# Two graph attention layers and a third: the first layer's bias moves from a product on TensorE to ScalarE's passes over the turned head

## The reference, cut to what matters

```
x = layernorm(x + gat2(elu(gat1(x)) ))       # block 0
x = layernorm(x + leaky(attention(x @ W) @ (x @ W)))   # block 1

gat(x):  xl   = (x @ W).reshape(N, H, F)
         e    = leaky_relu(asrc[s, h] + adst[d, h]), -1e9 where there is no edge
         attn = softmax over the sources s
         out  = sum over s of attn[s, d, h] * xl[s, h, :]   + bias
```

## Time and profile before

| what | value |
|---|---|
| median of 3 runs | 977.99 us (976.63 to 978.44) |
| the profiled execution, its own time | 977.93 us |
| span of the profiled execution | 976.1 us |
| TensorE busy (matmul) | 882.8 us, 90% |
| VectorE busy | 740.5 us, 76% |
| ScalarE busy | 684.9 us, 70% |
| GpSimd busy | 276.1 us, 28% |
| chain that ended last, by engine | TensorE 36%, VectorE 29%, ScalarE 24%, issue 9%, GpSimd 2% |

### The profile page before, as it was taken

How to read it: one execution, slowest core, us unless ns; L and a number is a source line. 1 busy time by engine, 2 the same in 40 slices (tenths; PEclk the granted TensorE clock), 3 DMA queues, 4 the chain that set the end, 5 groups by cost and what they waited for, 6 DMA issues and landing times.

```text
span 976.1 us, 17256 instructions
## 1 busy us (share of the span) xinstructions
PE 882.8 (90%) x6220; PEld 820.9 (84%) x6220; DVE 740.5 (76%) x1876; ACT 684.9 (70%) x1269; POOL 276.1 (28%) x255
## 2 busy tenths in 40 slices
PE   5687889999999999999999999999999999998653
PEld 4676879998999989898999989898999989897542
DVE  5657697888888887888888888888888888974430
ACT  2466858787786868787786868777786868775530
POOL 1001001124242314224242314224242314224353
PEclk9997999999999999999999999999999999999787
DMA  6303030202102030302102030302102010000000
GB/s 205 111 3 87 1 87 2 87 1 63 48 28 82 22 87 1 109 1 64 46 28 82 22 88 1 108 2 65 45 29 80 23 23 1 23 1 23 22 22 22
DMA packets 62716, 45.04 MB, mean 46 GB/s; under 512 B 35748, under 2 KB 54308, under 8 KB 62632
## 3 DMA queue, kind: packets, MB, share of 16 engines
q1 hardware_dynamic: 62632, 43.93, 15.3%
HBM read 27.14 MB, written 8.39 MB: 36 GB/s over the span
## 4 chain that ended last, share of the span: by engine, by line
PE 36%; DVE 29%; ACT 24%; issue 9%; POOL 2%; POOLq 0%; DMA 0%; SPq 0%; DVEq 0%; ACTq 0%
DVE junk L749 9%; PE bU L478 7%; PE bU L457 7%; PE bG L540 6%; PE bG L526 6%; ACT att L620 6%; ACT att L609 6%; ACT x L632 5%; DVE att L793 3%; PE bB L417 3%; DVE y_lo L786 3%; DVE low L762 3%; DVE y L774 3%; ACT att L624 2%; PE bU L468 2%
## 5 line engine op out<-in xcount | busy, mean ns | idle before, releaser
L749 DVE CUSTOM_DVE_ANT_0 junk<-mask_t,bA,val 128x512 bf16<-128x512 bf16 x320 | 219.8, 743 | 44.7 <-PE bA L417 38.2
L457 PE MATMUL bU<-val,att 128*128 128x129 f32 x2048 | 249.7, 275 | 3.3 <-DVE att L793 3.3
L457 PEld LDWEIGHTS bU<-val,att 128*128 128x128 f32 x2048 | 241.5, 192 | 5.7 <-issue 3.4
L793 DVE SCALAR_TENSOR_TENSOR att<-mask_n,att 128x2048 f32<-128x2048 bf16 x80 | 183.4, 2292 | 81.3 <-ACT att L620 81.3
L609 ACT ACTIVATE att<-bB,val 128x512 f32<-128x512 f32 x320 | 202.4, 707 | 1.3 <-PE bB L417 1.3
L620 ACT ACTIVATE att<-att 128x2048 f32<-128x2048 f32 x80 | 155.2, 1940 | 0.7
L478 PE MATMUL bU<-val3s,att 128*128 128x256 f32 x512 | 118.0, 385 | 11.8 <-POOL val3s L372 11.3
L468 PE MATMUL bU<-val,att 128*128 128x257 f32 x512 | 119.9, 388 | 9.4 <-DVE att L793 9.4
L478 PEld LDWEIGHTS bU<-val3s,att 128*128 128x128 f32 x512 | 96.2, 192 | 27.0 <-issue 13.4
L468 PEld LDWEIGHTS bU<-val,att 128*128 128x128 f32 x512 | 96.6, 194 | 23.7 <-DVE att L793 9.9
L672 ACT COPY val<-bG 128x524 f32<-128x524 f32 x64 | 38.7, 604 | 108.6 <-PE bG L540 108.6
(11 more groups left out here) (87 smaller groups left out, 1585.4 us busy)
## 6 DMA issues: line engine op xcount, KB each, us to landing
adj_in<-in_adj_dram SPq DMA_DIRECT2D x16, 1024.0 KB, 5.8
x_in<-in_x_dram SPq DMA_DIRECT2D x16, 512.0 KB, 6.7
out_dram<-act SPq DMA_DIRECT2D x16, 512.0 KB, 2.9
mask_t<-mask_n SPq DMA_TRANSPOSE x64, 2.5
att<-in_L_gnn_W_dram SPq DMA_DIRECT2D x4, 128.0 KB, 3.1
att<-in_L_gnn_W_dram SPq DMA_DIRECT2D x1, 512.0 KB, 7.4
w<-in_L_gnn_W_dram SPq DMA_DIRECT2D x1, 256.0 KB, 7.6
att<-in_L_gnn_a_dram SPq DMA_DIRECT2D x1, 256.0 KB, 7.3
```

The source lines that it names most:

```text
L457: ins = nc.tensor.matmul(to[:, (d % 2) * FX:(d % 2 + 1) * FX], p[:, s, d * P:(d + 1) * P], val1[u.batch % 2][:, s, u.index // 2, values], ...
L749: nc.vector.tensor_tensor_reduce(junk[:, b] if u.row else att[u.slot % 3][:, b], mask_t[u.batch % 4][:, b], bA[:], 1.0, a_col(u, b) if u.r ...
L793: nc.vector.scalar_tensor_tensor(flat(p), mask_n[u.batch % 3][:, 0:NB * N], BIG, flat(p), ALU.add, ALU.min)\
```

## The change

The bias product goes, and with it `ones_r`, the prepared rows and `shift_bias_1`. The bias is loaded as one column per head (`bias1`, 128 x 4) by a DMA late in SP's queue. GpSimd writes the column of ones into val1 once per batch (`set_ones`), and the attention product of a head waits for it. The turning now takes the plain normalized head x1, two slots behind instead of three, at the end of TensorE's slot, after the second half of the product. ScalarE then reads the turned head from PSUM twice, with the bias as a column: exponential into e1 and rectified into r1 (`elu_parts`, three slots behind, at the end of the slot). VectorE's `elu` makes y1 = min(e1, 1) + r1, which is already turned. High and low part are made from y1 in SBUF, four slots behind. y1 has one buffer instead of two, and the bank of a turned head is freed by r1 instead of y_lo.

```diff
         u_uses = [(colsum_out, 2)]
         for g in range(FIRST, LAST + 1):
-            u, older = units.get(g - 1), head_at(g - 3)
+            u, older = units.get(g - 1), head_at(g - 2)
...
             if u:
-                u.use = len(u_uses), len(u_uses) + len(halves[0]) + (older is not None)
-            u_uses += halves[0]
+                u.use = len(u_uses), len(u_uses) + len(halves[0])
+            u_uses += halves[0] + halves[1]
             if older:
                 older.turn_use = len(u_uses)
-                u_uses.append((y_lo_ready, older.h + 1))
-            u_uses += halves[1]
+                u_uses.append((r1_done, older.h + 1))
@@ SP
-            b1_row = b1.rearrange("(o n) -> o n", o=1)
-            sp.dma_start(b1_in[0:1, :], b1_row).then_inc(b1_loaded, 16)
-            sp.dma_start(b1_in[32:33, :], b1_row).then_inc(b1_loaded, 16)
...
+            with nc.allow_non_contiguous_dma(reason="a column for each head"):
+                sp.dma_start(bias1[:], b1.rearrange("(h p) -> p h", p=P)).then_inc(b1_loaded, 16)
             sp.dma_start(bias2[:], b2.rearrange("(o a) -> o a", o=1).to_broadcast([P, DO])).then_inc(w23_in, 16)
@@ GpSimd
-            nc.gpsimd.memset(ones_r[:].bitcast(F32), 1.0).then_inc(consts, 1)
-            nc.gpsimd.memset(bias1[:].bitcast(F32), 0.0).then_inc(const0, 1)
...
+            def set_ones(n):
+
+                pool.wait_ge(val1_ready, (n + 1) * NB)
+                columns = val1[n % 2][:].rearrange("p b g n -> p (b g) n")[:, :, 0:HC].rearrange("p q (c n) -> p q c n", n=FX)
+                nc.gpsimd.memset(columns[:, :, :, F:FX], 1.0).then_inc(ones_ready, 1)
...
+                if pos == 0 and 0 <= n < B:
+                    set_ones(n)
@@ TensorE
             def turn_head(u):
                 to = u_bank(u.turn_use)
-                pe.wait_ge(y1_done, u.h + 1)
+                pe.wait_ge(x1_done, (u.h + 1) * NB)
...
                 pe.wait_ge(prob_done, u.r + 1)
+                pe.wait_ge(ones_ready, u.batch + 1)
...
-                    nc.tensor.matmul(to, ones_r[:], bias1[:, g], start=True, stop=False)
...
                 if before:
                     attend(before, 0)
-                if oldest:
-                    turn_head(oldest)
                 if after and after.row:
                     targets_row(after)
...
                 if before:
                     attend(before, 1)
+                if older:
+                    turn_head(older)
                 if later:
                     sources_row(later)
@@ ScalarE
-            def elu_exp(u):
-                act.wait_ge(x1_done, (u.h + 1) * NB)
+            def elu_parts(u):
+
+                act.wait_ge(x1_turned, u.h + 1)
+                act.wait_ge(b1_loaded, 16)
                 if u.h:
                     act.wait_ge(y1_done, u.h)
-                nc.scalar.activation(e1[:], x1[u.h % 2][:], ACT.Exp, bias=neg_one[:]).then_inc(e1_done, 1)
+                turned, bias = bU[u.turn_use % 4][:], bias1[:, u.index:u.index + 1]
+                nc.scalar.activation(e1[:], turned, ACT.Exp, bias=bias).then_inc(e1_done, 1)
+                nc.scalar.activation(r1[:], turned, ACT.Relu, bias=bias).then_inc(r1_done, 1)
 
             def high_part(u):
-                act.wait_ge(y_turned, u.h + 1)
+                act.wait_ge(y1_done, u.h + 1)
...
-                nc.scalar.copy(y_hi[:, u.index], bU[u.turn_use % 4][:]).then_inc(y_hi_ready, 1)
+                nc.scalar.copy(y_hi[:, u.index], y1[:]).then_inc(y_hi_ready, 1)
...
+                turned = head_at(g - 4)
...
+                if turned and pos == 2:
+                    high_part(turned)
                 if this:
                     leaky(this, (0, 1))
...
-                if oldest:
-                    high_part(oldest)
+                if turned and pos != 2:
+                    high_part(turned)
                 if pos == 4 and third:
                     values_3_out(n - 2, (2, 3))
-                if older:
-                    elu_exp(older)
+                if oldest:
+                    elu_parts(oldest)
@@ VectorE
             def elu(u):
                 dve.wait_ge(e1_done, u.h + 1)
-                if u.h >= 2:
-                    dve.wait_ge(y_turned, u.h - 1)
-                nc.vector.scalar_tensor_tensor(y1[u.h % 2][:], e1[:], 1.0, x1[u.h % 2][:], ALU.min, ALU.max)\
-                    .then_inc(y1_done, 1)
+                dve.wait_ge(r1_done, u.h + 1)
+                if u.h:
+                    dve.wait_ge(y_lo_ready, u.h)
+                nc.vector.scalar_tensor_tensor(y1[:], e1[:], 1.0, r1[:], ALU.min, ALU.add).then_inc(y1_done, 1)
...
-                nc.vector.tensor_tensor(y_lo[:, u.index], bU[u.turn_use % 4][:], y_hi[:, u.index], ALU.subtract)\
-                    .then_inc(y_lo_ready, 1)
+                nc.vector.tensor_tensor(y_lo[:, u.index], y1[:], y_hi[:, u.index], ALU.subtract).then_inc(y_lo_ready, 1)
...
-            shift_bias_1()
             fold_1()
...
-                if last_head:
-                    low_part(last_head)
+                if turned and pos == 2:
+                    low_part(turned)
...
-                if oldest and pos != 1:
-                    low_part(oldest)
-                if older:
-                    elu(older)
+                if turned and pos != 2:
+                    low_part(turned)
+                if oldest:
+                    elu(oldest)
                 if pos == 1 and 0 <= n - 2 < B:
                     norm_stats(n - 2, 0, res1, res1_done, NB, stats1, moments1)
```

More of the change, by code:

```diff
@@ L114, in gat_kernel @@
         e1 = sb("e1", [P, N])
-        y1 = [sb(f"y1_{i}", [P, N]) for i in range(2)]
+        r1 = sb("r1", [P, N])
+        y1 = sb("y1", [P, N])
         y_hi = sb("y_hi", [P, KH, N], F32R)
@@ L335, in _ @@
             nc.gpsimd.memset(val2[:, :, DX:DX + 1], 1.0).then_inc(consts, 1)
-            pool.wait_ge(const0, 2)
-            nc.gpsimd.memset(bias1[0:1, :, 0:HC].rearrange("p g (c n) -> p g c n", n=FX)[:, :, :, F:FX].bitcast(F32), 1.0)\
-                .then_inc(consts, 1)
+            pool.wait_ge(const0, 1)
             nc.gpsimd.affine_select(out=ident[:], in_=ident[:], compare_op=ALU.not_equal, fill=1.0, base=0,
                                     pattern=[[-1, P]], channel_multiplier=1).then_inc(consts, 1)
-            pool.wait_ge(consts, 8)
+            pool.wait_ge(consts, 6)
             nc.gpsimd.tensor_scalar(ident_big[:], ident[:], BIG, 1.0, ALU.mult, ALU.mult).then_inc(consts, 1)
-            pool.wait_ge(consts, 9)
+            pool.wait_ge(consts, 7)
             def norm_scale(m, which, moments_sem, var_sem, rstd_sem):
@@ L536, in values_1 @@
                     to = g_bank(g)[:, 0:HX]
-                    nc.tensor.matmul(to, ones_r[:], bias1[:, g], start=True, stop=False)
                     for k in range(KD):
                         for i, (left, right) in enumerate(((x_hi, w1_hi), (x_hi, w1_lo), (x_lo, w1_hi))):
-                            ins = nc.tensor.matmul(to, left[:, k, nodes], right[:, k, g], start=False,
-                                                   stop=(k == KD - 1 and i == 2))
+                            ins = nc.tensor.matmul(to, left[:, k, nodes], right[:, k, g],
+                                                   start=(k == 0 and i == 0), stop=(k == KD - 1 and i == 2))
                     g_free[g] = ((val1_ready, n * NB + b + 1),)
@@ L545, in weight_sums @@
             def weight_sums():
-                pe.wait_ge(folded, 2 * KD * H + G + 2 * KH)
+                pe.wait_ge(folded, 2 * KD * H + 2 * KH)
                 for k in range(KH):
@@ L692, in _ @@
                 if g == -1:
-                    act.wait_ge(folded, 2 * KD * H + G + 2 * KH)
+                    act.wait_ge(folded, 2 * KD * H + 2 * KH)
                     nc.scalar.copy(w2_hi[:], w2).then_inc(w2_hi_ready, 1)
                 third_layer = units.get(g - 2) if pos == 2 else None
+                if turned and pos == 2:
+                    high_part(turned)
                 if this:
@@ L856, in fold_1 @@
                                         w1_hi[:].rearrange("p k g n -> p (k g n)"), ALU.subtract).then_inc(w1_lo_ready, 1)
-            def shift_bias_1():
-                dve.wait_ge(consts, 9)
-                dve.wait_ge(b1_loaded, 32)
-                for g in range(G):
-                    to_hi, to_lo = (bias1[q:q + 1, g, 0:HC].rearrange("p (c n) -> p c n", n=FX)[:, :, 0:F] for q in (0, 32))
-                    from_hi, from_lo = (b1_in[q:q + 1, g * HW:(g + 1) * HW].rearrange("p (c n) -> p c n", n=F)
-                                        for q in (0, 32))
-                    nc.vector.tensor_scalar(to_hi, from_hi, 1.0, None, ALU.add).then_inc(bias1_ready, 1)
-                    nc.vector.tensor_scalar(to_lo, from_lo, 1.0, None, ALU.add).then_inc(folded, 1)
-                    folds[0] += 1
-                    dve.wait_ge(folded, folds[0])
```

(3 more changed lines are left out.)

24 lines of the change are left out of this document (11 added, 13 removed).

## The result

The changed kernel takes **1029.1 us** (1025.5 to 1030.8, 4 runs) against 977.7 (976.6 to 978.4, 4 runs) of the kernel before: ratio 1.052, interval 1.051 to 1.054. The prediction had the sign and the two waits, but forecast +21 where the profiled spans show 1029.0 - 976.1 = +52.9. It lies well outside the range of 980 to 1006.

A forecast was written before the change was run, and what follows sets the result against it. TensorE was taken as nearly the bound (busy 53.6 of 55 us); per batch +1.75-0.86+0.73 = +1.62, 21.8 over the batches, last fourth quarter +0.6, start and batch 1 -1.5, total +20.9: 998.8 us, range 980 to 1006.

The forecast's parts named there:

- the two waits: TensorE waits 2.0 us for the rectified pass at layer 2's fourth quarter, about 1.3 for b_t at head 2's targets row.
- M4 to M5: Stretch from values_3's end to layer 2's fourth quarter: bank held until the rectified pass ends, 1.75 us more per batch.
- M1 to M3: Stretch from values_1's end to head 3's targets row: VectorE's elu ahead of the statistics, 0.73 us more per batch.
- M2: Mark on TensorE's queue: targets row of head 2, forecast to move from 7.38 to 8.5 us behind values_1's end.
- M1: Mark on TensorE's queue: end of values_1 of block 0, where the second half of the third layer's product starts.
- M3 to M4: Stretch from head 3's targets row to the end of values_3 of blocks 2 and 3: no change, within 0.05 us.
- M5 to M1: Stretch from layer 2's fourth quarter to values_1's end: shorter gap at the targets row, two products gone, 0.86 us less.
- The start: Before the steady part: two loads leave SP's queue, -0.6 us, and eight uncovered products go, -1.8 us.
- the first three: Rivals: only TensorE's work counts (961 us, 8%); only the bank waits (984, 10%); only VectorE's order waits (976.5, 6%).
- the shared port: Rival: a GpSimd operation holds VectorE's low part of head 3 by 1.0 us each batch; 1013 us, 4%.
- M4: Mark on TensorE's queue: end of values_3 of blocks 2 and 3.
- M5: Mark on TensorE's queue: start of the fourth quarter of layer 2's product.

The follow-up runs named there:

- e1_fill: Changed kernel with 16 idle-time transposes into a free bank ahead of the fourth quarter's bank wait; 1018.3 us, ratio 1.041.
- e6_no_relu: Changed kernel without ScalarE's rectified pass, VectorE taking e1 twice; 991.0 us, ratio 1.015.
- e10_pass_old_order: Kernel of before without the bias product, GpSimd adding the bias in place, plus only ScalarE's rectified pass per head; 978.4 us, ratio 1.001.

## Why the prediction was right in kind and wrong in size

**Which steps held.** *M4 to M5* named the right bank, the right releaser, and a wait of 2.0; measured 2.03 to 2.04 in twelve batches. *M1 to M3* named VectorE's order; M2 was to move to M1+8.5 and moved to 555.82 - 547.27 = 8.55, with a wait of 1.24. M1 to M3 was to grow by 0.73 and is 18.87, +0.83. M3 to M4 is 9.81, +0.08. *M5 to M1*, forecast 8.29, is 8.07. The start came out: the first tops stand at 30.66 instead of 32.61, 1.95 sooner, and the load of the bias as columns (issued in 0.72 us) delays the fold behind it by 0.11. The rivals came out wrong. For the first three, both waits are there; for the shared port, y_lo takes 0.66 to 0.78 (one of 64, at 86.51, takes 1.21).

**The step that failed first** is in *M4 to M5*: "It waits 2.0 us, and M4 to M5 grows by 1.75". The wait was costed as its own length and the products behind it at the durations of before, taken at full clock. In seven of twelve batches they ran partly at 1.2 GHz, 1.7 to 1.9 us more each. e1_fill, which leaves the bank's release as late and takes away only the idleness, gives 10.8 us back. In the stretch that I had read the longest wait of TensorE was 0.65 us, so nothing there showed what comes behind a longer one. The end of the same trace did:

```profile
919.65 10.04 PE L468 MATMUL bU<-val,att 128*128 128x257 f32 x32 [5.94 <-DVE att L793]
```

These are 32 products that take 6.9 us at full clock (16 hold the queue 3.47), and the granted clock behind that wait is 0.50 from 919.6 to 924.5.

**The second** is the size of the same term. M4 to M5 was forecast at 19.67 and is 20.37. ScalarE's and VectorE's timelines of the batch show the 0.70:

```profile
594.97 0.71 ACT L644 ACTIVATE e<-bU,bias 128x512 f32<-128x512 f32 x1
595.55 0.71 ACT L645 ACTIVATE r<-bU,bias 128x512 f32<-128x512 f32 x1
596.12 2.45 ACT L610 ACTIVATE att<-bB,val 128x512 f32<-128x512 f32 x4
```

```profile
577.78 0.69 DVE L783 SCALAR_TENSOR_TENSOR y<-e,r 128x512 f32<-128x512 f32 x1 [1.11 <-ACT r L645]
...
587.07 0.69 DVE L794 TENSOR_TENSOR y_lo<-y,y_hi 128x512 fp32r<-128x512 f32 x1
587.88 0.75 DVE L783 SCALAR_TENSOR_TENSOR y<-e,r 128x512 f32<-128x512 f32 x1
```

The pass itself takes its 0.57 of the queue, as estimated (595.55 to 596.12). But TensorE starts 0.20 behind that, at 596.32, where I took 0.05 for the semaphore. And "up to ScalarE's exponential of head 2 the chain stays as it is" was wrong by 0.55 (it ends at M4+19.60 instead of 19.05): the first y stands at M4+1.83, 0.22 later than the 493.01 - 491.40 = 1.61 of before; the second y starts 0.81 behind y_lo where it was 0.60, because y has one buffer now and `elu` waits for the signal of the y_lo just ahead of it on the same engine; and it takes 0.07 longer. Each is small, and each lies on a chain that is walked once per batch. In the prediction's terms, the pass was let into M4 to M5 once and its turn ahead of the first y was taken as paid for by the low part that leaves; e6_no_relu and the chain below have it on the path twice. The other pieces miss by +0.10 (M1 to M3), +0.08 (M3 to M4) and -0.22 (M5 to M1), which nearly cancel: the batch is 0.7 longer than forecast, as much as this one term.

**The third** is that the sum had the waits of the steady batches only. Ahead of the fourth batch's M5 I had put next to nothing, since there "TensorE already waits"; measured 9.0. Where TensorE waits for a chain of ScalarE and VectorE, that chain is the bound, and what the new pass adds to it adds to the time. Timeline of TensorE after, two targets rows of the third batch:

```profile
136.72 1.11 PE L419 MATMUL bB<-ident,b_t 128*128 128x128 f32 x4 [3.79 <-DVE b_t L775]
...
148.56 1.12 PE L419 MATMUL bB<-ident,b_t 128*128 128x128 f32 x4 [4.14 <-DVE b_t L775]
```

Four transposes take 1.11 us here and 0.65 at full clock, so the clock has a part in it as well. Without the pass the same two rows stand at 129.53 and 140.12 and take 0.65, and M5 follows 10.3 us sooner. How the 9.0 divide between chain and clock was not separated; nor were the 5.4 us at the end.

**What the chain of waits says.** The engines of a batch close a loop. Pieces of it in the chain that ended last of the kernel after, one ahead of M2 and then from M4 on (start, us, what):

```profile
549.17 0.59 ACT r L645
...
577.11 0.59 ACT r L645
...
577.78 0.69 DVE y L783
578.47 1.31 DVE stats L834 x4
...
580.22 1.14 ACT x L633 x4
...
583.01 1.82 ACT att L621
...
584.86 2.29 DVE att L800
587.15 0.61 DVE y_lo L794
...
587.88 0.12 DVE y L783
...
588.82 1.14 ACT x L633 x4
...
595.68 0.59 ACT r L645
```

From M4 to M5, some 20 us, the chain leaves TensorE altogether and runs between ScalarE and VectorE, twice through `r`, twice through y; a third `r` stands ahead of M2. Three passes of 0.57 are 1.71, and the run without the pass gave 1.66 a batch. The chain of the kernel before ran over the same stretch through the same two engines, only without `r`:

```profile
492.41 0.68 DVE y_lo L786
493.10 0.60 DVE y L774
...
495.45 1.14 ACT x L632 x4
```

So a TensorE that is busy 53.6 of 55 us had a second path of nearly the same length beside it, and the pass went onto that one. This is how I read why the loss did not vanish with TensorE's waits: they were the shadow of this loop. The runs with the statistics first and with elu's passes ahead removed 0.8 and 1.5 us of a wait and left the batch at 57.13 and 57.23; giving the bank back earlier gave 0.72, and the run without the pass 1.66 for a bank wait only 0.59 shorter. That a loop sets the batch of 57.12 fits these runs; that every piece of it is necessary for it was not tried.

## What to carry to other kernels

A wait of a nearly full TensorE costs its length plus what the clock does behind it: look at the granted clock of the stretch behind each new wait, and price both cases. When an engine's wait is removed and the batch does not shorten, follow the chain that ended last through the other engines; the pass that was called cheap because its engine is busy 70% may stand in that chain several times. And before trading work from a full engine to a free one, run the removal alone and the addition alone: here the first was worth 7.7 us and GpSimd could take the bias for nothing. In the old order ScalarE's pass would only have eaten that gain (978.4); the new order cost 21.5 us by itself and 50.7 together with the pass.

## What the runs showed of the hardware

- The clock fell behind waits of 2.04 us in seven of twelve batches and not in the five others, with the same work ahead and behind. In the profiled executions it fell behind none of 1.45 us (e6_no_relu, e10_pass_old_order), nor of the 1.24 to 1.38 at targets rows. In the third batch the rows right behind 3.79 and 4.14 us ran at 1.2 GHz after the change. In e6_no_relu those right behind 3.81 and 3.10 ran at 2.4 GHz, and the clock fell about 1 us later: it was 0.50 from 131.5 to 133 and from 142 to 144, behind rows at 129.53 and 140.12. So of waits of 2 us the length alone does not tell, and a fall can come some time behind the wait.
- A handover from ScalarE to TensorE took 0.20 us from the end of the pass's share of the queue to the first product; one from ScalarE to VectorE 0.21 (577.57, where ScalarE goes on, to 577.78).
- GpSimd is slowed as well: the scaling of L3's values, four operations, takes 3.15 us at 593.93 after and 2.72 at 453.99 before, and L350's mean rises to 1693 ns from 1584 of the same operation before, where y_lo now reads both of its operands from SBUF. In e10_pass_old_order, where y_lo still reads one from PSUM, the two are 2.73 us and 1586 ns, which points to y_lo and not to y or to the new pass. The Trainium skill (GPSIMD Engine Reference, Specifications) names contention over the SBUF interfaces that the two engines share where VectorE has two SBUF inputs, without saying who is slowed; `low` in the earlier trace rows shows it on VectorE, these rows on GpSimd.
